# Eight zero products left out of the prologue of a fused attention and soft-mixture kernel

## Chip, cores, metric

The kernel runs on one core of one Trainium2 chip. The metric is the device time of one execution in microseconds; the time before is the median of three runs.

## What is computed

The input is 16 sequences of 256 tokens with 128 features. Layer norm comes first, and its result feeds two branches whose outputs are added to the input.

```python
x = L0_attn_x                                  # (16, 256, 128)
xn = _layernorm(x, axis=-1)
x = x + _L0_attn_ref(xn, Wqkv, bqkv, Wout, bout, omega, quad_nodes, quad_weights)
      + _L0_ffn_ref(xn, gamma_x, gamma_slot, slot_embeds, w1, w2)
# attention branch, 16 heads of 8:
#   qkv = xn @ Wqkv + bqkv; q and k per head -> unit length -> exp features (64 of them)
#   causal linear attention: out = sum(qf.kf v) / sum(qf.kf); then @ Wout + bout
# expert branch, 8 experts x 64 slots = 512 slots:
#   logits = rms_norm(xn, gamma_x) . rms_norm(slot_embeds, gamma_slot)
#   dispatch = softmax over tokens, combine = softmax over slots
#   slots = dispatch^T xn; processed = gelu(slots @ w1) @ w2; out = combine @ processed
```

## The kernel before

One sequence (256 tokens, two tiles of 128) is a row; 16 rows are run in order. Each engine has its own instruction list, written out by hand: a prologue for what is needed once, then a function `row` called for every row. There is no planner: the order of an engine's work is the order of the calls, and semaphores tie the engines together. Row 0 runs with some of its inputs made in the prologue, and in each row part of the previous row's attention (its context sums, output projection) and part of the next row's preparation are mixed in.

The prologue, engine by engine, as far as the change touches it:

- SyncE (queue SP) starts the loads: half of the first x tile, Wqkv, the slot embeddings (`se_rows`), the broadcasts of gamma_slot and gamma_x (`gs_bc`, `gx_bc`), omega, the second x tile, then w1, w2, Wout. It later starts the transposed load of the feature stack (`turn_stack`) and the x tiles of later rows.
- GpSimd clears `omega_f` and `stack`, makes the identity (`ident`, lines 417 to 421) and the causal mask, clears one tile of `s_sb` (line 428, semaphore `s_zero`), and then writes the negated identity (line 433), which brings `pool_id` to 5. Later it scales the slot embeddings (`se_g`, line 476) and prepares omega (lines 482 to 492).
- VectorE computes the layer norm of row 0 (`ln_stats`, `ln_apply`, which writes `xg`), splits Wqkv into a high and a low part, forms `xt_lo` (line 741), multiplies the two gammas (line 866, `gs_rt`), clamps the squared norms of the slot embeddings (line 869), a few small constants (lines 873 to 876), the reciprocal root by Newton (lines 879 to 883), the qkv bias (line 750), q and k norms, the normalised embeddings `se_n` (line 890), their low part `se_lo` (line 899), the stack's low part (line 329), and the layer norm of row 1.
- ScalarE copies x's transposes (`xt_high`, line 545), squares the slot embeddings (line 622, four times with a read of the accumulator each), takes the roots, and copies `se_hi` (line 638).
- TensorE: the zero products, x's transposes (`transposes`, line 973), the qkv product (`qkv_product`, through `three`, line 964: high x high, high x low, low x high), the transposes of `se_n` (line 1199), zero products again. Row 0 then begins with the logits (`logits_tokens`, line 964 too), the transposes of row 1's x, the turned logits (`logits_turned`, line 1106), the shift by the maxima (`shift`, lines 1117 and 1125), the projections onto the random features (`project`, line 1000) and the slot sums (line 1133).

The zero products multiply the identity by a tile of zeros into the score banks `p_s`, which nobody reads before they are written again. Line 773 on VectorE is the clip of a projection, line 815 the maxima of the turned logits, line 825 the reciprocal of the slot sums' weights, which begins the slots' normalisation. Line 600 on ScalarE is the GELU, line 1163 the product behind it.

Of the kernel before, what the change touches and what calls it, by code (L numbers as in the profile page):

```python
# [92 lines left out]
def build(nc, x, Wqkv, bqkv, Wout, bout, omega, nodes, weights, gamma_x, gamma_slot, slot_embeds,  # L93
          w1, w2, out):
    with ExitStack() as ctx:
        def sb(name, shape, dt=F32):
            return ctx.enter_context(nc.sbuf_tensor(name, shape, dt))

        def pb(name, shape):
            return ctx.enter_context(nc.psum_tensor(name, shape, F32))  # L100

        def sem(name):
            return ctx.enter_context(nc.semaphore(name))


        ident = sb("ident", [128, 128])
# [54 lines left out]
        s_sb = sb("s_sb", [128, 8, 2, 384])  # L161
# [20 lines left out]
        p_s = pb("p_s", [128, 2, 512])  # L182
# [31 lines left out]
        s_zero = sem("s_zero")  # L214
# [745 lines left out]
        def _(pe):  # L960
# [7 lines left out]
            def transposes(b):  # L968
                after(pe, xg_ok, count(b, 1, 1))
                after(pe, prs_ok, count(b, 2, -3))  # L970
                dst = p_t if is_row(b, 1) else x01
                for j in range(TILES):
                    mm = nc.tensor.transpose(dst[:, 0, 128 * j:128 * j + 128], xg[:, b[1], j, 0:C], ident[:, :])
                mm.then_inc(tr_ok, 1)
# [213 lines left out]

            b0 = (0, 0)
            pe.wait_ge(pool_id, 5)  # L1190
            pe.wait_ge(s_zero, 1)
            for u in range(2):
                nc.tensor.matmul(p_s[:, u, 0:384], ident[:, :], s_sb[:, 0, 0, :], start=True, stop=True)
            transposes(b0)
            pe.wait_ge(wq_split, 2)
            qkv_product(b0)
# [1 line left out]
            for c in range(NCH):  # L1198
                mm = nc.tensor.transpose(x01[:, 1, 128 * c:128 * c + 128], se_n[:, c, :], ident[:, :])
            mm.then_inc(se_t, 1)  # L1200
            for u in range(2):
                nc.tensor.matmul(p_s[:, u, 0:384], ident[:, :], s_sb[:, 0, 0, :], start=True, stop=True)
            pe.wait_ge(vz_const, 2)

            def row(b, first, nxt, nxt2):
# [85 lines left out]
```

## Time and profile before

| what | value |
|---|---|
| median of 3 runs | 471.46 us (470.74 to 471.81) |
| profiled execution | 468.73 us |
| its span | 467.0 us (1.73 us lie around it) |
| TensorE busy | 435.5 us, 93% of the span |
| VectorE busy | 373.7 us, 80% |
| ScalarE busy | 314.7 us, 67% |
| GpSimd busy | 196.6 us, 42% |
| mean granted TensorE clock | 0.998 |

The busy shares are means over the span; the prologue is its first 25 us or so, in which TensorE is idle for more than half of the time. The chain of waits, followed back from the last instruction, says which engine's work sets the end, stretch by stretch. Matmuls are pipelined: the time between the starts of two of them is their pace, while the time given for one includes its tail. PE is TensorE, PEld its weight loads, DVE VectorE, ACT ScalarE, POOL GpSimd, and a q behind a name its queue.

### The profile page before, as it was taken

The numbers are of one execution on the slowest core, as the hardware profiler recorded it, in microseconds if no ns is written. First come the engines' busy times: TensorE is split into PE (matmuls) and PEld (weight loads), VectorE is DVE, ScalarE is ACT, GpSimd is POOL, SyncE is SP. The second block draws the span as 40 slices with busy tenths as digits, with TensorE's granted clock in tenths as the row PEclk, the third lists the DMA queues.
The fourth block names the chain that finished last, engine by engine and source line by source line (L and its number), as shares of the span: only waits on it lengthen the run. The fifth ranks groups of instructions, "written<-read, shape, count | busy, mean of one in ns | idle before, by whom it ended". The sixth has DMA issues, their size and how long they took to land.

```text
span 467.0 us, 15993 instructions
## 1 busy us (share of the span) xinstructions
PE 435.5 (93%) x5708; PEld 359.3 (77%) x5708; DVE 373.7 (80%) x949; ACT 314.7 (67%) x577; POOL 196.6 (42%) x286
## 2 busy tenths in 40 slices
PE   2578999999999999999999999999999999999993
PEld 1357878788877878888788888788887878888782
DVE  4888788888888789887978888887988889677462
ACT  1638675767767576776767667686766768676761
POOL 6645354334435334443533443353334335334220
PEclk9999999999999999999999999999999999999999
DMA  3231002020200202020010202011020201102000
GB/s 94 63 67 36 20 8 58 15 53 19 47 22 10 46 11 52 16 45 22 18 38 11 56 11 45 22 25 31 11 56 11 45 11 34 24 4 58 1 10 15
DMA packets 45387, 14.50 MB, mean 31 GB/s; under 512 B 35216, under 2 KB 45200, under 8 KB 45360
## 3 DMA queue, kind: packets, MB, share of 16 engines
q1 hardware_dynamic: 44800, 13.87, 14.0%
q8 instruction: 17, 0.28, 0.3%
q10 hardware_dynamic: 432, 0.26, 0.2%
q0 software_dynamic: 128, 0.01, 0.1%
q14 instruction: 10, 0.08, 0.1%
HBM read 3.57 MB, written 2.10 MB: 12 GB/s over the span
## 4 chain that ended last, share of the span: by engine, by line
PE 68%; DVE 22%; issue 5%; ACT 2%; POOL 1%; DVEq 1%; POOLq 0%
PE x L964 11%; PE p_s L1015 8%; PE x L1172 7%; PE x L1184 6%; PE p_t L1015 6%; DVE arg L773 6%; PE p_s L1027 5%; PE x L1163 4%; PE x L1027 3%; PE x L1106 3%; DVE slot_v L828 3%; PE p_s L1000 2%; PE x L1141 2%; DVE s_sb L779 2%; PE x L1117 2%
## 5 line engine op out<-in xcount | busy, mean ns | idle before, releaser
L472 POOL TENSOR_TENSOR s_sb<-s_sb,causal 128x256 f32<-128x256 f32 x96 | 68.1, 730 | 112.4 <-ACT s_sb L566 110.4
L561 ACT ACTIVATE feat<-arg,f_bias 128x512 f32<-128x512 f32 x128 | 87.8, 717 | 0.2
L773 DVE TENSOR_SCALAR arg<-p_s,f_low,f_high 128x512 f32<-128x512 f32 x64 | 48.8, 803 | 13.5 <-PE p_s L1000 13.5
L1015 PEld LDWEIGHTS p_s<-feat 64*64 64x64 f32 x1024 | 38.6, 132 | 18.2 <-issue 16.6
L773 DVE TENSOR_SCALAR arg<-p_t,f_low,f_high 128x512 f32<-128x512 f32 x64 | 49.9, 800 | 0.0
L316 POOL TENSOR_TENSOR qk_sq<-qkv 128x512 f32<-128x512 f32 x15 | 15.6, 1040 | 81.2 <-DVE qkv L750 81.2
L1015 PE MATMUL p_s<-feat 64*64 64x256 f32 (+3 forms) x1024 | 49.5, 309 | 0.0
L1015 PE MATMUL p_t<-feat 64*64 64x256 f32 (+3 forms) x1024 | 46.1, 296 | 0.0
L466 POOL TENSOR_TENSOR s_sb<-s_sb,causal 128x512 f32<-128x512 f32 x30 | 37.5, 1272 | 16.8 <-ACT s_sb L572 16.8
L1015 PEld LDWEIGHTS p_t<-feat 64*64 64x64 f32 x1024 | 41.6, 133 | 1.5
L1133 PEld LDWEIGHTS x<-xg,disp 128*128 128x128 f32 x256 | 29.8, 191 | 7.9 <-ACT disp L588 7.9
L815 DVE TENSOR_REDUCE maxima<-x 128x2 bf16<-128x512 f32 x32 | 20.6, 686 | 16.5 <-PE x L1106 16.5
L1163 PE MATMUL x<-w_sb,hid_t 128*128 128x128 f32 x256 | 32.8, 281 | 0.6 <-ACT hid_t L600 0.6
L1133 PE MATMUL x<-xg,disp 128*128 128x129 f32 x256 | 32.8, 281 | 0.2
L1172 PEld LDWEIGHTS x<-w_sb,hid_t 128*128 128x128 f32 x256 | 29.8, 191 | 4.2 <-issue 4.2
L600 ACT ACTIVATE hid_t<-x 128x1024 f32<-128x1024 f32 x32 | 32.6, 1020 | 0.4 <-PE x L964 0.2
L1172 PE MATMUL x<-w_sb,hid_t 128*128 128x128 f32 x256 | 32.8, 281 | 0.0
L1163 PEld LDWEIGHTS x<-w_sb,hid_t 128*128 128x128 f32 x256 | 29.8, 191 | 1.9 <-ACT hid_t L600 0.8
L1184 PE MATMUL x<-proc,comb_t 128*128 128x129 f32 x256 | 31.2, 275 | 0.0
L1184 PEld LDWEIGHTS x<-proc,comb_t 128*128 128x128 f32 x256 | 29.8, 191 | 0.0
L779 DVE TENSOR_TENSOR s_sb<-p_s,causal 128x384 f32<-128x384 f32 x48 | 26.3, 547 | 4.2 <-PE p_s L1015 4.2
L964 PE MATMUL x<-slot_hi,w_hi 128*128 128x512 f32 x64 | 26.9, 421 | 0.7 <-DVE slot_lo L833 0.7
(159 smaller groups left out, 1029.2 us busy)
## 6 DMA issues: line engine op xcount, KB each, us to landing
out_dram<-out_sb SPq DMA_DIRECT2D x32, 64.0 KB, 2.2
xin<-in_L_attn_x_dram SPq DMA_DIRECT2D x31, 64.0 KB, 2.4
se_rows<-n_L_ffn_slot_embeds_dram SPq DMA_DIRECT2D x1, 256.0 KB, 5.7
w_f<-in_L_ffn_w_dram SPq DMA_DIRECT2D x1, 256.0 KB, 3.0
w_sb<-in_L_ffn_w_dram SPq DMA_DIRECT2D x1, 256.0 KB, 3.0
stack_t<-stack SPq DMA_TRANSPOSE x16, 4.3
bqkv_bc<-in_L_attn_bqkv_dram ACTq DMA_DIRECT2D x1, 192.0 KB, 5.3
wqkv_f<-in_L_attn_Wqkv_dram SPq DMA_DIRECT2D x1, 192.0 KB, 4.1
```

The lines of the kernel that those rows point to most:

```text
L466: pool.tensor_tensor(v, v, m, ALU.mult).then_inc(mb_ok, 1)
L472: pool.tensor_tensor(v, v, m, ALU.mult).then_inc(mb_ok, 1)
L561: nc.scalar.activation(feat[:, p % 4, :], arg[:, p % 4, :], ACT.Exp, bias=f_bias[:, 0:1]).then_inc(fe_ok, 1)
L773: nc.vector.tensor_scalar(arg[:, p % 4, :], bank, f_low[:, 0:1], f_high[:, 0:1], ALU.max, ALU.min).then_inc(cl_ok, 1)
L779: nc.vector.tensor_tensor(s_sb[:, p, 0, :], (p_s, p_t)[p % 2][:, 0, 0:384], causal[:, :], ALU.mult).then_inc(ea_ok, 1)
L964: mm = nc.tensor.matmul(dst, a, w, start=start and i == 0, stop=stop and i == 2, skip_group_check=True)
L1015: mm = nc.tensor.matmul(dst[rows:rows + 64, u, o:o + hi - lo], f[:, T + keys:T + keys + 64], f[:, lo:hi], start=True, stop=True, skip_grou ...
L1027: mm = nc.tensor.matmul(dst[32 * q:32 * q + 32, j, 384:512], vw[:, b[1], kt, QUADS * a + q, :], s_sb[:, p, q % 2, o:o + 128], start=(kt == ...
L1133: mm = nc.tensor.matmul(x01[:, half, 129 * (c % 2):129 * (c % 2) + 129], disp[:, j, 128 * c:128 * c + 128], xg[:, b[1], j, :], start=(j == ...
L1163: nc.tensor.matmul(x01[:, c // 2, o:o + 128], hid_t[:, m, 128 * c:128 * c + 128], w2_sb[:, m, :], start=(m == 0 and c % 2 == 0), stop=Fals ...
L1172: mm = nc.tensor.matmul(x01[:, c // 2, o:o + 128], hid_t[:, m, 128 * c:128 * c + 128], w2_sb[:, m, :], start=False, stop=(m == 3), skip_gr ...
L1184: mm = nc.tensor.matmul(x23[:, 0, 129 * j:129 * j + 129], comb_t[:, c, 128 * j:128 * j + 128], proc[:, c, :], start=(c == 0 and j == 0), s ...
```

## The change

TensorE's prologue loses both groups of four products (two calls each, which the chip runs as four instructions) and the wait on `s_zero`. GpSimd still clears the tile, and the wait for `pool_id` to reach 5 stays.

```diff
             b0 = (0, 0)
             pe.wait_ge(pool_id, 5)
-            pe.wait_ge(s_zero, 1)
-            for u in range(2):
-                nc.tensor.matmul(p_s[:, u, 0:384], ident[:, :], s_sb[:, 0, 0, :], start=True, stop=True)
             transposes(b0)
             pe.wait_ge(wq_split, 2)
             qkv_product(b0)
@@
             for c in range(NCH):
                 mm = nc.tensor.transpose(x01[:, 1, 128 * c:128 * c + 128], se_n[:, c, :], ident[:, :])
             mm.then_inc(se_t, 1)
-            for u in range(2):
-                nc.tensor.matmul(p_s[:, u, 0:384], ident[:, :], s_sb[:, 0, 0, :], start=True, stop=True)
             pe.wait_ge(vz_const, 2)
```

## Rows read from the trace of the kernel before

**Rows 1.** The page, part 4: shares of the chain by engine.
```profile
PE 68%; DVE 22%; issue 5%; ACT 2%; POOL 1%; DVEq 1%; POOLq 0%
```

**Rows 2.** Chain of waits, first 60 us: start us, us, engine tile line.
```profile
8.29 2.93 PE p_s L1193 x4
11.22 0.44 PE x L973 x2
...
12.07 1.17 ACT junk L622 x8
...
13.27 0.92 DVE small L869
...
15.20 1.15 DVE qkv L750 x2
...
27.14 0.67 PE x L1106 x4
...
27.83 1.30 DVE maxima L815 x2
...
29.18 0.62 PE x L1117 x8
29.80 0.44 PE x L1125 x4
30.24 0.33 PE p_s L1000
...
30.60 2.25 DVE arg L773 x3
...
33.38 0.09 DVE slot_rs L825
...
41.46 2.05 PE x L1163 x16
```

**Rows 3.** Timeline, TensorE: start us, us, engine line op out<-in.
```profile
12.63 0.66 PE L964 MATMUL x<-wqkv_hi,xt_hi 128*128 128x384 f32 x1 [0.98 <-DVE xt_lo L741]
...
14.37 0.52 PE L964 MATMUL x<-wqkv_hi,xt_lo 128*128 128x384 f32 x1
...
18.74 1.11 PE L1199 MATMUL x<-ident,se_n 128*128 128x128 f32 x4 [3.85 <-DVE se_n L890]
19.65 2.77 PE L1202 MATMUL p_s<-s_sb,ident 128*128 128x384 f32 x4
...
23.95 0.63 PE L964 MATMUL x<-se_hi,xt_hi 128*128 128x512 f32 x1
24.38 0.50 PE L964 MATMUL x<-se_lo,xt_hi 128*128 128x512 f32 x1
24.72 0.40 PE L964 MATMUL x<-se_hi,xt_lo 128*128 128x512 f32 x1
...
30.75 2.05 PE L1133 MATMUL x<-xg,disp 128*128 128x129 f32 x16
...
50.10 0.39 PE L964 MATMUL x<-se_hi,xt_hi 128*128 128x512 f32 x1
50.33 0.40 PE L964 MATMUL x<-se_lo,xt_hi 128*128 128x512 f32 x1
```

**Rows 4.** Timeline of all engines, prologue.
```profile
3.25 0.43 SPq L366 DMA_DIRECT2D gx_bc<-in_L_ffn_gamma_x_dram  x1
...
12.45 0.28 DVE L866 SCALAR_TENSOR_TENSOR gs_rt<-gs_bc,gx_bc 128x128 f32<-128x128 f32 x1
...
12.87 1.28 POOL L476 TENSOR_TENSOR se_g<-se_rows,gs_rt 128x512 f32<-128x512 f32 x1 [4.36 <-issue]
...
20.16 2.69 POOL L491 TENSOR_TENSOR omega_st<-omega_f,omega_st 16x512 f16<-16x512 f32 x2
```

**Rows 5.** DMA view: issues, KB each, us from issue to landing.
```profile
gx_bc<-in_L_ffn_gamma_x_dram SPq DMA_DIRECT2D x1, 64.0 KB, 7.3
```

**Rows 6.** Windows: stretch, length, busy (x) PE PEld DVE ACT POOL, clock, DMA share, GB/s.
```profile
13.00:14.00 1.00, 1.00 (x4) 1.00 (x4) 0.73 (x1) 0.23 (x2) 1.00 (x1) 1.00 0.14 33
```

## The prediction

> **What bounds the kernel now.** I read the chain of waits on the page first: over the whole span TensorE holds 68% of it and VectorE 22% [rows 1]. So in the middle of the kernel the time is TensorE's, and an edit in the prologue is worth whatever it moves the point at which the steady part begins, as long as the work in between follows. I then read the same chain for the first 60 us, piece by piece, since the change is only there [rows 2]. The reader is to see four stretches. (a) Up to the first zero product at 8.29 us the chain is GpSimd's, ending in the negated identity. (b) The first four zero products stand on the chain with 2.93 us, and directly behind them x's two transposes (0.44), ScalarE's copy of them, and ScalarE's eight instructions on the slot embeddings (1.17). The latter are not about x at all: they stand behind x's copy in ScalarE's queue. (c) From 13.27 to about 27 us the chain is VectorE's own queue. (d) Row 0 begins: the turned logits (from 27.14), the maxima, the shift and the first projection on TensorE (29.18 to 30.57), VectorE's clips, and from 41.46 us on TensorE without a break. The second four zero products are nowhere on the chain.
>
> The third view is TensorE alone in order of time [rows 3]. Its lesson is the pace. Successive 512-column products start 0.43 us apart at 23.95 and 24.38, 0.34 apart next, and 0.23 apart at 50.10 and 50.33. 0.43 us for 512 columns is TensorE at 1.2 GHz, 0.23 close to 2.4 GHz: the engine changed level at about 24.6 us. The six qkv products at 12.63 to 14.37, 0.35 us apart for 384 columns, were at the lower level as well. So were the first zero products.
>
> **The clock column and a page.** The windows view says 1.00 for the granted clock in this early stretch [rows 6], where the pace is half; it shows no change before the first one it records, so here the pace must be trusted. If the column were right, nothing below about the clock would apply and the edit would be a clean gain (the first rival). The Trainium skill, "TensorE: Matmul & The Clock Gate", Part 1, "What's actually happening", says that the throttled state is the default and activity releases it; by that sentence the zero products are not useless work. The pace in this trace agrees with it, the column does not.
>
> **Part 1: the first four zero products and the wait on the zeroed tile.** The wait on the identity (the fifth count, GpSimd's negation) stays; x was normalised before that. The transposes therefore start at 8.29 instead of 11.02, 2.73 us earlier [rows 2]. They cost the same, being at the lower level in both. The zeroed tile was ready before the identity, so dropping that wait is worth nothing.
>
> ScalarE's copy and the eight instructions on the slot embeddings follow: they end at about 10.5 instead of 13.24. VectorE then meets something else. Its scale product for the slot embeddings (line 866) needs gamma_x, whose broadcast load is issued at 3.25 [rows 4] and takes 7.3 us [rows 5]: it lands at 10.55. Before, line 866 began at 12.45 and this was hidden; now it can only begin at 10.55, a shift of 1.90. GpSimd's product se_g starts 0.14 us behind the end of line 866 and takes 1.28: 12.87 to 14.15 before, 10.97 to 12.25 after. In the trace the tiny clamp of line 869 ran from 13.27 to 14.19, that is, it ended with se_g although it is four columns wide [rows 2, 4]. The Trainium skill, "SBUF — State Buffer", section "SBUF: two separate sides", calls the port pair of VectorE and GpSimd an exclusive lock that the first holds for its whole instruction; the 0.92 us agrees with that, and my sum would be the same if it were some other cause. Either line 869 or the small instructions behind it will again wait for se_g. So the VectorE chain moves by 1.9, not by 2.73. Upper bound of this shift: 2.73, if no small instruction is held. Lower bound: 1.5, if one more of them meets a GpSimd instruction for part of its length (0.4 of the 0.92). I take 2.0, a little over the 1.9, since the order clamp-first is possible.
>
> Nothing else stands in the way of the shift. TensorE's qkv products end before VectorE asks for them in either case. GpSimd's preparation of omega, whose last part is issued at 20.16 and ends at 22.85 [rows 4], is wanted only by the first projection at 30.24 [rows 2]. SyncE's queue, which carries the stack's transposed load and the next x tiles, waits for VectorE and moves with it. The second x tile was loaded long before.
>
> **Part 2: the second four zero products.** They run from 19.65 to 22.42, and the six logits products, which need VectorE's se_lo, come at once behind them and end at 25.12 [rows 3]. No piece of the chain is theirs, nor the logits'; I count their removal at nothing by itself. But they close the gap in TensorE's work: with the transposes of the slot embeddings (from 18.74 [rows 3]) they make one unbroken run of TensorE up to the rise at 24.6, 5.9 us after its start. What of shorter runs? The one from 8.29 to 11.66 lasted 3.37 us and the one from 12.63 to 14.89 lasted 2.3 us, and neither brought the rise [rows 2, 3]. Afterwards the runs are: two transposes (0.65), six qkv products (2.3), four transposes (1.1), six logits products (2.6 at the lower level), two transposes, eight turned logits (1.8). All are shorter than the 3.37 that did nothing. So I expect TensorE still at 1.2 GHz when row 0 reaches its TensorE stretches.
>
> The logits themselves end at 25.12 and the turning starts 2.0 us later, so 0.3 more is hidden. The stretches on the chain are not:
> - Turned logits: 128-column products start about 0.11 us apart (16 in 2.05 less the last one's tail [rows 3]). The first four must end before VectorE reduces them: + 4 x 0.11 = 0.45. The second four take 0.88 at the lower level against one reduction of 0.65 (half of 1.30): + 0.2.
> - Shift and first projection: starts 0.46 + 0.43 + 0.23 = 1.1 us apart in all (0.62 and 0.44 in the chain, 0.33 with tails [rows 2]); at half the clock + 1.0.
>
> Together + 1.65. VectorE's first clip therefore begins at 30.60 - 2.0 + 1.65 = 30.25, 0.35 earlier than before.
>
> **Part 3: until the clock rises.** From the shift on TensorE is dense: that starts at 29.18 - 2.0 + 0.65 = 27.8. Counting from there the 3.37 us that weren't enough and the 5.9 us that were, the rise comes between 31.2 and 33.7; I take 32.5. The 16 slot-sum products start at 30.75 - 0.35 + 0.2 = 30.6. To 32.5 that makes 8.6 products at 0.22; the other 7.4 take 0.8: ready at 33.5 with 0.2 tail. VectorE would want them at 33.38 - 0.35 = 33.0 [rows 2]. So 0.5 is lost, and the rest of row 0 stands at -0.35 + 0.5 = + 0.1. With the rise at 31.2: 2.7 products slow, 13.3 x 0.11 = 1.5, ready at 32.9: nothing lost, -0.35. With the rise at 33.7: 14.1 products slow, ready at 34.1: 1.1 lost, + 0.7. From 41.46 on the chain is TensorE's and carries this difference to the end.
>
> **Sum.** Gain 2.0 (bounds 1.5 and 2.7); clock on the chain of row 0 1.65; slot sums 0.5 (bounds 0 and 1.1). Net + 0.1, from -1.1 (2.7 and 0) to + 1.3 (1.5 and 1.1). The sum is made against the profiled execution, 468.73 us with a span of 467.0 and 1.73 around it: 468.8. The median of the timed runs is 471.46, 2.7 above the profiled one; some of them may have had a late rise already with the zero products, which would favour the change a little. I put the forecast at 471.4.
>
> **Rivals.**
> 1. The clock costs nothing: it rises during the logits anyway, or the slower TensorE is hidden. For it: the clock column. Against it: the pace at 12.63 to 24.4, and that four of the eight turned logits, the shift and the projection stand on the chain. It gives the whole shift, 1.9 to 2.7: 468.8 to 469.6. Chance 0.20.
> 2. The gain is larger than its price: the clamp escapes se_g and the rise is early, -0.35 - 0.7 = about -1.1, or the timed runs of before suffer from a late rise. 470.0 to 470.5. Chance 0.12.
> 3. The other side: a late rise. The place is row 0's slot sums and the six qkv products behind them, which feed VectorE's bias and, over GpSimd's squares and ScalarE, the GELU. Each us at the lower level there costs half a us. From a rise at about 34.5 the second half of the slot sums comes 1.2 late and what stands behind decides: + 1.0 to + 2.0, 472.4 to 473.5. For it: the density of row 0 has small gaps. Against it: slack of 0.8 or so behind. Chance 0.16.
> 4. The zero products do not matter in either sense (both groups hidden): excluded for the first group by the chain.
>
> **How the numbers follow.** The likeliest case, gain and clock cancelling, has 0.52 and its own range is 470.5 to 472.4. A difference of 0.2% (0.94 us) is about what a measurement of this kernel can tell from none. Faster by more: rivals 1 and 2, less the half of 2 near the border, plus a little of the likeliest: 0.30. Slower by more: rival 3 and the likeliest's upper edge: 0.18. Same: 0.52. The range must reach to rival 1 on the low side and into rival 3: 469.2 to 472.8.
>
> **What would show it.** x's transposes at 8.3 and the qkv bias at about 13.2 instead of 15.20 (if at 12.5, the whole shift came through). Line 866 starting at 10.6. The logits products 0.43 apart to the last; eight turned logits taking 1.8 instead of 1.09, the four wide shift products 0.21 apart. First clip near 30.2, slot sums over 2.7 us long, GELU's products starting at 41.5. The prediction is wrong if the pace is at 0.23 already in the logits, or if the clip begins below 29.5 or above 31.

## The result, and the profile after

The changed kernel takes 468.55 us at the median (466.44 to 469.93, 7 runs) against 470.77 us (469.67 to 471.81, 7 runs): 2.2 us faster between the medians, a ratio of 0.9947 with a 95% interval of 0.9921 to 0.9973. The forecast was no change that can be measured, 471.4 us with a range down to 469.2. The result lies below that range; over 12 further runs the ratio was 0.9960 (0.9940 to 0.9979).

The profiled execution hardly shows this: 468.81 us against 468.73, spans of 467.1 and 467.0. That is the first thing to explain. The chain of waits of the changed kernel, first 60 us (start us, us, engine tile line), beside [rows 2]:

```profile
8.30 0.70 PE x L973 x2
...
9.41 1.17 ACT junk L622 x8
...
10.60 0.18 DVE small L869
...
11.28 0.74 DVE small L879
...
12.36 1.15 DVE qkv L750 x2
...
24.39 1.98 PE x L1106 x8
...
26.40 0.70 DVE maxima L815
...
27.15 1.04 PE x L1117 x8
28.18 0.85 PE x L1125 x4
29.04 0.54 PE p_s L1000 x2
...
30.01 2.40 PE x L1133 x16
...
40.73 2.05 PE x L1163 x16
```

The qkv bias starts at 12.36 instead of 15.20: 2.84 earlier. The steady part (line 1163) starts at 40.73 instead of 41.46: 0.73 earlier. Of the 2.11 lost between them, 1.85 is gone when VectorE's first clip begins (29.61 against 30.60), on the turned logits, the shift and the projection. Another 0.15 goes by the third clip, behind the slot sums, and 0.11 behind that, where VectorE's line 759 takes 0.77 us and took 0.66. TensorE alone in order of time, beside [rows 3]:

```profile
22.08 0.63 PE L964 MATMUL x<-se_hi,xt_lo 128*128 128x512 f32 x1
...
24.39 1.97 PE L1106 MATMUL x<-ident,log_sb 128*128 128x128 f32 x8 [0.90 <-DVE log_sb L808]
27.15 1.04 PE L1117 MATMUL x<-neg_ident,maxima 128*128 128x128 bf16 x8 [0.79 <-DVE maxima L815]
27.98 1.06 PE L1125 MATMUL x<-neg_ident,maxima 128*128 128x256 bf16 x4
...
29.94 2.47 PE L1133 MATMUL x<-xg,disp 128*128 128x129 f32 x16
```

The turned logits take 1.97 us (1.09 before). The four wide shift products (line 1125) start 0.25 us apart, where it was 0.13 before. By this pace TensorE is at 1.2 GHz into the slot sums, which take 2.47 us and took 2.05. So far this is the mechanism of the prediction.

The remaining 0.8 us of the profiled execution goes in its tail. Windows of the changed kernel (stretch, length, busy of each engine, granted clock, DMA):

```profile
460.00:461.00 1.00, 0.06 (x1) 0.06 (x1) 0.85 (x5) 0.00 (x0) 0.00 (x0) 0.96 0.00 0
461.00:462.00 1.00, 0.63 (x2) 0.23 (x2) 0.00 (x0) 0.33 (x1) 0.00 (x0) 0.50 0.00 0
462.00:463.00 1.00, 0.90 (x4) 0.90 (x4) 0.00 (x0) 0.05 (x1) 0.00 (x0) 0.50 0.00 0
```

The clock fell at about 461, while TensorE waited for the last row's attention, and the last two groups of products (lines 1076 and 1082) cost 0.70 and 1.23 us on the chain. Before, the same stretch read 1.00 up to 464 and they cost 0.45 and 0.73. The change did not touch those lines. A comparison of two profiled executions therefore says nothing here to better than a microsecond; the experiments had to say where the 2.2 us come from.

### The profile page after: what moved, and what is told of

Same layout as the page of the kernel before. It is cut to its first block, busy times and chain, and to the rows that moved or that the text cites. A ratio compares the mean times of both kernels' runs of the same rounds, so it can differ in the third digit from the quotient of the medians.

```text
span 467.1 us, 15977 instructions
## 1 busy us (share of the span) xinstructions
PE 433.9 (93%) x5700; PEld 359.1 (77%) x5700; DVE 374.8 (80%) x949; ACT 315.2 (67%) x577; POOL 196.0 (42%) x286
## 3 DMA queue, kind: packets, MB, share of 16 engines
HBM read 3.57 MB, written 2.10 MB: 12 GB/s over the span
## 4 chain that ended last, share of the span: by engine, by line
PE 69%; DVE 22%; issue 5%; ACT 2%; POOL 1%; DVEq 1%; POOLq 0%
PE x L964 11%; PE p_s L1015 8%; PE x L1172 7%; PE x L1184 6%; PE p_t L1015 6%; DVE arg L773 5%; PE p_s L1027 5%; PE x L1163 4%; PE x L1106 4%; PE x L1027 3%; DVE slot_v L828 3%; PE p_s L1000 2%; PE x L1141 2%; DVE s_sb L779 2%; PE x L1117 2%
## 5 line engine op out<-in xcount | busy, mean ns | idle before, releaser
L1184 PE MATMUL x<-proc,comb_t 128*128 128x129 f32 x256 | 31.2, 275 | 0.0
```

Of the source, the lines that this page charges most:

```text
L1184: mm = nc.tensor.matmul(x23[:, 0, 129 * j:129 * j + 129], comb_t[:, c, 128 * j:128 * j + 128], proc[:, c, :], start=(c == 0 and j == 0), s ...
```

## Experiments

**The kernel before, again.**

> The kernel before once more, unchanged. Theory A (the time of one execution depends on when TensorE's clock rises and falls relative to the program, which differs from execution to execution): the profiled span differs from 467.0 by 0.5 to 3 us, the rise (512- or 384-column pace) is not at 24.6 us, and the difference is found in row 0 or in the tail. Theory B (the profiled execution and the timed ones differ by something else): pace changes at 24.6 +- 0.3 again and the timed runs still lie 2 us above the profile's 468.73. The ratio to before is 1.000 within its interval in both.

Measured: 0.9998 (0.9978 to 1.0017), so the two sets agree, but neither is one number. Of the 35 executions of before that were run beside it, 9 took 468.7 to 468.9 us, 9 took 469.4 to 469.9, 2 took 470.5 to 470.7 and 15 took 471.4 to 471.7. The execution whose profile the prediction was built on (468.73) belongs to the lowest quarter. The profile of this run, 471.36 us, stands for the largest group. Its windows:

```profile
14.00:15.00 1.00, 0.00 (x0) 0.00 (x0) 0.67 (x7) 0.94 (x3) 0.00 (x0) 0.82 0.15 35
15.00:18.00 3.00, 0.00 (x0) 0.00 (x0) 2.83 (x7) 2.41 (x5) 1.74 (x2) 0.50 0.66 197
...
20.00:21.00 1.00, 1.00 (x3) 0.60 (x2) 0.90 (x4) 0.84 (x3) 1.00 (x1) 0.50 0.00 0
21.00:22.00 1.00, 0.91 (x2) 0.07 (x1) 0.97 (x5) 0.97 (x4) 0.93 (x2) 0.77 0.00 0
22.00:24.00 2.00, 1.63 (x6) 1.05 (x6) 1.97 (x5) 0.00 (x0) 1.83 (x4) 1.00 0.02 4
24.00:25.00 1.00, 0.00 (x0) 0.00 (x0) 0.93 (x4) 0.00 (x0) 1.00 (x5) 1.00 0.35 71
25.00:26.00 1.00, 0.44 (x2) 0.21 (x2) 1.00 (x4) 0.09 (x1) 1.00 (x1) 1.00 1.15 212
26.00:27.00 1.00, 0.05 (x1) 0.05 (x1) 1.00 (x5) 0.29 (x1) 0.85 (x3) 1.00 1.15 210
27.00:28.00 1.00, 1.00 (x8) 0.81 (x8) 0.59 (x2) 0.00 (x0) 1.00 (x1) 1.00 0.60 156
28.00:29.00 1.00, 0.05 (x2) 0.01 (x1) 1.00 (x3) 0.00 (x0) 0.82 (x2) 0.64 0.03 7
29.00:30.00 1.00, 1.00 (x9) 0.97 (x10) 0.81 (x6) 0.36 (x1) 0.00 (x0) 0.50 0.00 0
...
35.00:36.00 1.00, 1.00 (x8) 1.00 (x8) 0.51 (x2) 0.00 (x0) 0.00 (x0) 0.94 0.00 0
```

The clock is up early, falls in the idle prologue (0.50 from 14.6 to 21.5 us), rises in the second group and falls again at about 28.3, in the pause ahead of the shift. The second figure of a row is TensorE's busy time: from 24 to 29 us it reads 0.00, 0.44, 0.05, 1.00 and 0.05. The turned logits still run at full pace; shift, projection and slot sums then run at half clock, and the chain of the same execution reads:

```profile
26.95 0.67 PE x L1106 x4
...
28.99 1.04 PE x L1117 x8
30.03 0.85 PE x L1125 x4
...
31.85 3.57 PE x L1133 x16
...
43.75 2.05 PE x L1163 x16
```

43.75 against 41.46 in [rows 2]: with both groups of zero products in place this execution is 2.3 us later, and 2.5 counted from the qkv bias, which began 0.2 us earlier (15.00). Theory A stands.

**One group at a time.** The three kernels of this part and the one above ran side by side.

```diff
-            pe.wait_ge(s_zero, 1)
-            for u in range(2):
-                nc.tensor.matmul(p_s[:, u, 0:384], ident[:, :], s_sb[:, 0, 0, :], start=True, stop=True)
             transposes(b0)
...
             mm.then_inc(se_t, 1)
+            pe.wait_ge(s_zero, 1)
             for u in range(2):
                 nc.tensor.matmul(p_s[:, u, 0:384], ident[:, :], s_sb[:, 0, 0, :], start=True, stop=True)
```

That is the first of them, with only the first group out. The second leaves the first group and takes these last two lines away; the third is the first one with the removed lines put back behind the call of `qkv_product(b0)`.

> Only the first four zero products are left out, the second four stay. Theory A (the edit's gain is the first group's 2.8 us on the chain, its price is the missing second group through the clock): qkv bias starts near 12.4, the whole prologue 2.8 earlier, rise during the logits, and 2.5 to 2.8 us faster than before, so better than the changed kernel where the profile shows the early rise. Rival (the second group is worth nothing): the same time as the changed kernel, 2.2 us faster than before.

Measured: 467.63 us, 0.9952 (0.9931 to 0.9973). Its profiled execution had the clock up in row 0 and shows the full shift: qkv bias 12.39, shift at 26.45, line 1163 at 38.72, 2.74 before the 41.46 of [rows 2]. But its 12 executions spread from 466.26 to 469.26, and its ratio cannot be told from that of the changed kernel. The time is the rival's (2.2 us), the profile is Theory A's.

> Only the second four zero products are left out, the first four stay. Theory A: the prologue is unmoved (qkv bias at 15.20), TensorE comes into row 0 at half pace, first clip near 32.3 instead of 30.60 and the GELU's products near 43.5 instead of 41.46: 1.5 to 2.3 us slower than before. Rival (the clock rises in time anyway or its cost is hidden): 0 to 0.3 us from before.

Measured: 471.68 us, 1.0034 (1.0016 to 1.0051), and a spread of only 0.75 us (471.41 to 472.16). Line 1163 starts at 44.01, the turned logits take 1.98 on the chain and the slot sums 3.20. With the prologue unmoved, no execution reached before's lower groups. So with the first group in place the second does buy something, 1.6 us by the ratio. The profiles point to the clock: turned logits 1.98 us on the chain without it, 0.67 (four of the eight) with it, in both profiles of before. Theory A stands, at the lower end of its size.

> The first four zero products stand behind the qkv product instead of ahead of x's transposes, where TensorE is idle for 3.7 us in the changed kernel; the second four stay. Theory A: the shift of 2.8 us comes through as in the changed kernel, the run from the qkv product on is long enough for the rise to come by about 15 us or in the second group, and row 0 is at full pace: 2.8 to 3.0 us faster than before. Rival (activity this early does not carry over, the clock falls again before row 0): like the one with only the first group out.

Measured: 469.10 us, 0.9967 (0.9946 to 0.9989), less than the expectation and nearer to its rival. In its profile the zero products at 12.54 us still run at half pace (2.76 us for four) and those at 17.23 at full pace (1.46). The granted clock falls at about 26.4 and reads 0.50 from 27 to 32: the clock had come up early and was lost again in row 0. In the same profile the qkv bias started at 13.20, not 12.4; gamma_x had taken 7.8 us to land. The expectation of 2.8 to 3.0 us missed both.

**Filling the pauses of row 0.** TensorE stands still before and after the transposes of row 1's x and behind the turned logits. The three products put there are zero products of 256 columns into a bank that is written again.

```diff
             if first:
+                fill(1, 256)
                 transposes(b1)
+                fill(1, 256)
...
             logits_turned(b)
+            if first:
+                fill(1, 256)
```

> The kernel before with three further zero products of 256 columns in row 0: ahead of and behind the transposes of row 1's x, and behind the turned logits, where TensorE otherwise stands still between 25 and 29 us. Theory A (the timed runs of before differ because the clock, once risen, falls again in that pause in some executions): the slow groups at about 469.7 and 471.5 disappear and the runs lie at 468.6 to 468.9, median about 1.3 us faster than before. Rival (the spread has another source): same median, same spread of 3 us.

Measured: 468.69 us, 0.9961 (0.9946 to 0.9975), 12 executions between 468.60 and 469.44 beside 17 of before between 468.60 and 471.58. Between the medians of the two sets that is 2.6 us, by the ratio 1.8. Nine of the 12 lie at 468.60 to 468.89, so the lowest group has become the rule and the upper ones are gone. The turned logits and the shift run at full pace:

```profile
27.03 1.09 PE L1106 MATMUL x<-ident,log_sb 128*128 128x128 f32 x8 [0.71 <-DVE log_sb L808]
...
29.06 0.62 PE L1117 MATMUL x<-neg_ident,maxima 128*128 128x128 bf16 x8 [0.51 <-DVE maxima L815]
```

The edit only gives TensorE work in the pauses of row 0, and the spread went with it: nearly all of the spread of before is the clock from there on.

> The kernel with only the first group out, and the same three products in row 0. Theory A: first clip near 28 us in nearly every execution, runs at 465.9 to 466.8, 3.5 us faster than before at the median and over 1 us faster than with only the first group out. Rival (the products get in the way of the transposes and of the shift, or the clock is low before): no faster than 467.6.

Measured: 466.65 us (466.35 to 467.01), 0.9916 (0.9895 to 0.9937). As expected in size. One detail is not: line 1163 starts at 39.39, 2.07 and not 2.8 before the 41.46, because the qkv bias starts at 13.12. Rows of VectorE and of GpSimd's product se_g in this kernel:

```profile
10.77 0.29 DVE L866 SCALAR_TENSOR_TENSOR gs_rt<-gs_bc,gx_bc 128x128 f32<-128x128 f32 x1 [0.90 <-DMA gx_bc<-in_L_ffn_gamma_x_dram]
11.20 0.17 DVE L869 TENSOR_SCALAR small<-small 128x4 f32<-128x4 f32 x1
11.28 1.25 DVE L873 TENSOR_SCALAR node_b<-node_b 128x2 f32<-128x2 f32 x1
...
12.62 0.15 DVE L879 SCALAR_TENSOR_TENSOR small<-small 128x4 f32<-128x4 f32 x1
13.12 1.14 DVE L750 SCALAR_TENSOR_TENSOR qkv<-x,small,bqkv_bc 128x384 f32<-128x384 f32 x2
...
11.21 1.30 POOL L476 TENSOR_TENSOR se_g<-se_rows,gs_rt 128x512 f32<-128x512 f32 x1 [2.79 <-DVE gs_rt L866]
```

Line 866 waits 0.90 us for gamma_x, and then a small VectorE instruction, here line 873 with two columns, takes 1.25 us and ends with se_g, as the prediction said.

These two kernels ran side by side and differ by the first group alone, with the clock up in row 0 in the profiles of both: 468.69 against 466.65, 2.04 us. That is the shift without the clock's spread, and the forecast had 2.0.

> As the one before, with TensorE kept busy in the whole prologue behind x's transposes: 2 products of 128 columns behind them, 3 of 384 behind the qkv product, 3 of 384 behind the embeddings' transposes. Theory A: clock up by about 14 us and never down again, all runs within 1 us at 465.9 to 466.9. Rival (more is no better, the pauses of row 0 alone decide): equal to the kernel with row 0 filled.

> As the dense one, with 1, 3 and 1 products of 128 columns in TensorE's pauses behind the last row's context sums, context transposes and attention transposes. Theory A (the clock also falls in the tail in some executions, which costs up to 0.8 us, as in the changed kernel's profile): 0.3 to 0.8 us faster than the dense one at the median, spread smaller. Rival (the tail's products delay what stands behind them): 0.2 slower than the dense one.

Measured: 466.68 us, 0.9918 (0.9896 to 0.9940), and 466.64 us, 0.9919 (0.9898 to 0.9941). More products in the prologue buy nothing beyond the three in row 0: the rival. In the tail the clock stayed up longer (mean granted 0.999 against 0.996) and the time did not move; the expectation of 0.3 to 0.8 is wrong. The two profiles show why for their executions: lines 1076 and 1082 cost 0.45 and 0.73 us on the chain in both, so there was nothing to win. The clock of the dense kernel fell only behind them.

> The changed kernel with the three products of 256 columns in row 0's pauses, and nothing in front of the logits. Theory A: they lengthen the run that begins with the logits, so the clock rises by about 26 us in part of the executions and later in the others, but doesn't fall again: 467.0 to 467.8 at the median, 0.5 to 1 faster than the changed kernel and still 0.5 behind the one that keeps the second group. Rival (the second group is needed at all): 468.5 as the changed kernel.

Measured: 466.57 us (466.34 to 467.08), 0.9924 (0.9899 to 0.9948). Better than expected: with the three short products the whole second group is needless. In the profile the second product (0.60 us, the first 1.05) and the turned logits (1.09) are at full pace already.

**Which of the three.** Each is the changed kernel with part of them.

> The changed kernel with two of the three products of 256 columns alone, those around the transposes of row 1's x. They join the logits and the turned logits into one run from 20.3 to 26.4. Theory (what the changed kernel lacks is a run long enough for the rise): about as good as with all three, 466.5 to 467.2. Rival (what it lacks is work in the pause behind the turned logits): 468 to 469.

> The changed kernel with only the third product of 256 columns, behind the turned logits. Theory (the run before row 0's shift is the cause): little, 467.8 to 468.8. Rival: as good as with all three, 466.6.

Measured: with the two around row 1's transposes 466.85 us (466.05 to 467.23), 0.9916 (0.9894 to 0.9938); with the third alone 467.40 us (466.63 to 468.20), 0.9934 (0.9911 to 0.9957). The changed kernel, beside them, had 468.46. The two do nearly all. The third helps more than its expectation allowed, but its profile can't say why, since the clock came up ahead of it:

```profile
23.11 0.63 PE L964 MATMUL x<-se_hi,xt_lo 128*128 128x512 f32 x1
23.82 0.69 PE L973 MATMUL p_t<-ident,xg 128*128 128x128 f32 x2
25.40 1.09 PE L1106 MATMUL x<-ident,log_sb 128*128 128x128 f32 x8 [0.89 <-DVE log_sb L808]
```

The logits and the transposes are at half pace, the turned logits at full pace, and up to there the kernel is the changed one. In the changed kernel's own profile the same instructions, at nearly the same distances, left the clock down (1.97). So the work that TensorE did just before doesn't settle whether the clock comes up.

**The changed kernel, again.**

> The changed kernel once more, unchanged. Theory A: its executions spread too, from 466.4 where the clock is up in row 0 to about 469.9 where it stays low until behind the slot sums; median 468 to 469, and the profile shows the rise at another place than 30.8 us or the same start-to-start times doubled up to it. Rival (the changed kernel has one single course, and what spreads is elsewhere): the same clock course again.

Measured: 468.46 us, 12 executions from 466.55 to 470.04. Its profiled one took 469.88: qkv bias at 12.83 and line 1163 at 42.07, with the slot sums at half pace for most of their length:

```profile
24.86 1.97 PE L1106 MATMUL x<-ident,log_sb 128*128 128x128 f32 x8 [0.90 <-DVE log_sb L808]
...
30.40 3.35 PE L1133 MATMUL x<-xg,disp 128*128 128x129 f32 x16
33.51 0.42 PE L964 MATMUL x<-wqkv_hi,xt_hi 128*128 128x384 f32 x1
```

Theory A stands here too: line 1163 comes 1.34 us later than in the first profile, 0.47 of it from the later qkv bias and the rest from the slot sums (3.35 against 2.47). The end gives only 1.1, as the first profile had lost more in its tail.

**What gates the prologue.** The edits stand on the kernel with row 0 filled: the move of gamma_x's load, the earlier transposes, and both.

```diff
             sp.dma_start(xin[0:64, 0, :, :], first[:, 0:4:3, :]).then_inc(d_x[0], 16)
+            spread(gx_bc, gamma_x, C).then_inc(d_gs, 16)
             sp.dma_start(wqkv_f[:, :], Wqkv).then_inc(d_qkv, 16)
...
-            spread(gx_bc, gamma_x, C).then_inc(d_gs, 16)
...
-            pe.wait_ge(pool_id, 5)
+            pe.wait_ge(pool_id, 3)
             transposes(b0)
+            pe.wait_ge(pool_id, 5)
```

> The kernel with row 0 filled, with the broadcast load of gamma_x issued right behind the first x tile instead of fifth. Theory (with x's transposes early, the scale product of line 866 is gated by gamma_x's landing in part of the executions, which is where the shift of 2.8 shrinks to 2.0): line 866 starts behind xt_lo at 9.8, at the latest; but se_g then runs from about 10.2 and can hold the clamp: 0 to 0.5 us faster than with row 0 filled, spread smaller. Rival (gamma_x gates nothing, the squares do): no difference, qkv bias at 12.4.

> The kernel with row 0 filled, where x's transposes wait for the identity alone (third count) and not for the mask and the negated identity. Transposes at about 7.5 instead of 8.3. Theory (gamma_x gates what follows): line 866 at its landing, 10.25 to 11.1, as before, no gain: within 0.3 us. Rival (the squares' chain is the gate): 0.8 us faster.

> Both of these together. Theory: transposes at 7.5, line 866 at about 9.0, se_g done by about 10.4, the constants' loads (landing near 10.4) next: qkv bias at 11.3 to 11.6, 0.8 to 1.0 us faster than with row 0 filled, 465.7 at the median. Rival (one of the loads of the constants or omega holds the chain at 12.3 anyway): no gain.

Measured: gamma_x first 467.56 us, 0.9943 (0.9922 to 0.9964); the earlier transposes 466.59 us, 0.9923 (0.9899 to 0.9948); both 467.71 us, 0.9948 (0.9931 to 0.9964). The earlier transposes are worth nothing (466.65 with row 0 filled alone), as expected with gamma_x as the gate: line 866 starts at 10.73 there, behind a wait of 0.88 for it. But moving the load costs 1 us, and both edits together are 1.1 us slower than the earlier transposes alone, where 0.8 to 1.0 of gain had been expected. In the profile with the load moved the others are late instead:

```profile
9.66 0.36 DVE L860 CAST wqkv_hi<-wqkv_f 128x384 fp32r<-128x384 f32 x1 [1.89 <-DMA wqkv_f<-in_L_attn_Wqkv_dram]
...
11.18 0.29 DVE L866 SCALAR_TENSOR_TENSOR gs_rt<-gs_bc,gx_bc 128x128 f32<-128x128 f32 x1 [0.23 <-DMA gs_bc<-in_L_ffn_gamma_slot_dram]
12.20 0.72 DVE L869 TENSOR_SCALAR small<-small 128x4 f32<-128x4 f32 x1 [0.73 <-ACT junk L622]
```

Against the profile with only the earlier transposes, gamma_x landed 4.7 us behind its issue instead of 7.4, but gamma_slot 8.0 instead of 6.0, the slot embeddings 8.2 instead of 7.4 and Wqkv 7.4 instead of 6.9; ScalarE's squares became the wait of line 869. That the loads of the first 10 us compete with each other fits this, but no run shows how. My expectation had counted the move as free.

## Why the prediction was wrong, point by point

The step that failed is the price of the clock, in Parts 2 and 3. It rests on a kernel before that has the clock up in row 0, so that the changed kernel must pay 1.65 us on row 0's chain and 0.5 at the slot sums for having lost it. This was read, correctly, from one execution. What the runs showed in its place: in the 471.36 us execution of before, which stands for the largest group (15 of 35), the clock is down in that very stretch. Shift and slot sums cost 1.04, 0.85 and 3.57 us on its chain, against 1.04, 0.85 and 2.40 in the changed kernel. Only the turned logits are still cheaper there (0.67). With the pauses of row 0 filled the groups above the lowest, 26 of the 35 executions, went away. So the changed kernel gives up something that before has in full in about a quarter of its executions. The sum mentioned this in one clause and gave it a small part of rival 2; it should have been the likeliest case, since the median stood 2.7 us above the profiled time and I had that number.

- **Chain, first group, transposes at 8.3.** Right: 8.30, and ScalarE's squares end at 10.6 as worked out (10.5).
- **Shift of the prologue, 2.0 (1.5 to 2.7).** Right at the median (2.04 between the two kernels with row 0 filled), but not constant. Measured on the qkv bias, against 15.20: 2.84 in the changed kernel's first profile, 2.37 in its second, and from 1.8 to 2.8 over the profiles of the kernels that only lack the first group ahead of the transposes. The first execution is above my upper bound. Gate and collision were the right ones: line 866 did wait for gamma_x, but it landed at 10.25 there, so the clamp (0.17) escaped se_g and line 879 met it (0.72). In other executions gamma_x lands up to 1.0 later; with row 0 filled, line 866 began 0.52 later and the qkv bias 0.76 later.
- **Clock, mechanism and size in a single execution.** Right: turned logits 1.97, the first clip 0.99 earlier (29.61 against 30.60), so a loss of 2.84 - 0.99 = 1.85 against 1.65. Up to the third clip another 0.15 goes at the slot sums, against 0.5. (The forecast read 0.43 between two starts of the shift where the trace has 0.53; nothing hangs on it.) By the Trainium skill, "TensorE: Matmul & The Clock Gate", Part 1, "What's actually happening", work releases the throttle; the trace agrees, as the windows of the 471.36 us execution read 0.50 behind the idle prologue and 1.00 behind the second group.
- **When the clock rises.** The prediction compared the lengths of TensorE's runs of work and expected the rise at 31.2 to 33.7. By the slot sums (2.47 and 3.35 us, 2.05 at full pace, 0.11 more for each slow product) an estimate puts it at 30.8 and 33.0 in the two profiles of the changed kernel, and with the third product alone it came before 25.4. The lengths were also misjudged: the logits and the transposes behind them, counted apart, came 0.1 us apart and ran for 3.7 us together. Nothing in these runs gives a length that decides.
- **What was not in it: the clock also falls.** The prediction asked only when it rises. The same page of the Trainium skill, under "HAM oscillation — how this bites in real kernels", tells of a kernel in which the wait for a DMA between bursts of products brings the throttle back each time. The windows agree in kind (0.64 at 28 to 29 us, behind pauses of 1.41, 1.14 and 0.95 us), and filling the pauses shows what it cost: 1.8 us by the ratio. Read for this, the 1.14 and 0.95 us pauses of row 0 were visible in the profile before.
- **Removing the second group costs nothing by itself.** Right only next to the first removal. Alone it cost 1.6 us; with the first group out too, no cost can be told (0.9952 and 0.9947 to 0.9960). A cause for this difference is not shown: the earlier prologue also changes when each burst comes.

So of the sum the shift is shown, 2.04 us with the clock held up and 1.8 to 2.8 over the profiles. The price of the clock against before is what remains to the measured 2.2 (1.9 and 2.5 by the two ratios): nothing that these runs can tell, not the 1.65 + 0.5 = 2.15 of the sum. The middle group of before at 469.7 was never profiled. It went away with the pauses filled, as the upper one did, but its course stays open.

The tail is open too. Line 1082 took 1.00 to 1.24 us on the chain in six of the seven profiles of kernels without products in row 0's pauses, and 0.72 or 0.73 in nine of the ten with them. Part of what filling row 0 is worth may lie there; no run separates it.

The version that beats both kernels is the changed one with the short products in row 0: 466.57 us with three of them and 466.85 with two, 0.8% below before, and 1.6 us below the changed kernel that ran beside the latter.

## What to carry to other kernels

Where a profiled execution lies outside the timed ones, find out first which kind of execution it is; its chain is true, but of that kind alone. Products that only keep TensorE busy belong into the pauses directly ahead of the work that stands on the chain, not at the head of the program, where they delay what waits behind them and where their effect can be lost in the next pause. And a prologue that became shorter meets the next gate at once: here a broadcast load, and moving that load only moved the wait.

## What the hardware showed that I had not expected

- The same program takes different courses through TensorE's two levels: in one execution of before the rise came at 24.6 us, in another the clock was up early, down from 14.6 to 21.5, up to 28.3 and down again to 35. The shift and the projection then cost 1.39 or 2.43 us on the chain, and the kernel 468.7 or 471.4.
- Three zero products of 256 columns, 0.6 us each at full pace and all in pauses, are worth 1.8 us by the ratio to a kernel of 470.
- The granted-clock column reads 1.00 ahead of the first change that it records, although 512-column products start 0.43 us apart there and 384-column ones 0.35 on average [rows 3, 6]. For the start of a program the pace is the witness.
- A VectorE instruction of four columns (line 869) took 0.17 us when it started ahead of GpSimd's se_g, in the changed kernel, and 0.92 when it started inside it [rows 2]. Not every small one is held: in the changed kernel line 876, with one column, took 0.14 us inside se_g.
